# A key-block offset between pairs of heads in a banded-attention tile loop

## The reference

```
q, k, v  = heads of (x @ W.T + b)
zq, zk   = q @ Wproj.T, k @ Wproj.T          # one scalar per row and head
bw       = softplus(log_bandwidth) + 1e-4
ctx[i]   = sum_j max(0, 1 - |zq[i] - zk[j]| / bw) * v[j]     / T
...                                           # expert layer: top 8 of 64 experts,
out      = routed experts + shared expert     # each of capacity 128
```

## Time and profile before

| | |
|---|---|
| median of three runs | 2455.28 us |
| the profiled execution | 2456.26 us |
| its span, first to last instruction | 2455.0 us |
| mean granted clock of TensorE | 0.906 of 2.4 GHz |
| PE busy | 1961.3 us (80%) |
| DVE busy | 2015.5 us (82%) |
| ACT busy | 1923.6 us (78%) |
| POOL busy | 999.9 us (41%) |

### The profile page before, as it was taken

One profiled execution on the slowest core, in us unless ns is written; L12 is line 12 of the kernel. 1 busy time (PEld: TensorE's weight loads), 2 busy tenths in 40 slices (PEclk: granted clock), 3 DMA queues, 4 the chain that ended last, 5 costly groups with the idle time before them and its releaser, 6 DMA issues.

```text
span 2455.0 us, 30185 instructions
## 1 busy us (share of the span) xinstructions
PE 1961.3 (80%) x11666; PEld 779.4 (32%) x11666; DVE 2015.5 (82%) x2895; ACT 1923.6 (78%) x1242; POOL 999.9 (41%) x356
## 2 busy tenths in 40 slices
PE   7788889789669889886788889778898884899920
PEld 4433233233112223221222322112232333677720
DVE  5497888797999998999998989998999986644348
ACT  2398998898999999999999999999999970122223
POOL 1020110100335367364284466342574371276754
PEclk9899999899889999998999999888999995788965
DMA  6315244335120212131202030312111018478779
GB/s 220 131 61 197 84 156 149 122 106 201 57 103 11 88 31 82 41 110 43 95 31 80 20 107 20 123 49 83 50 58 56 20 46 222 108 188 185 179 197 314
DMA packets 182039, 259.26 MB, mean 106 GB/s; under 512 B 22280, under 2 KB 162184, under 8 KB 173704
## 3 DMA queue, kind: packets, MB, share of 16 engines
q1 hardware_dynamic: 167408, 237.83, 29.1%
q0 software_dynamic: 12288, 18.88, 4.5%
q10 hardware_dynamic: 2200, 0.60, 0.1%
HBM read 187.25 MB, written 70.03 MB: 105 GB/s over the span
## 4 chain that ended last, share of the span: by engine, by line
PE 35%; ACT 28%; DVE 24%; POOL 5%; issue 4%; DMA 3%; SPq 1%; DVEq 0%; POOLq 0%; ACTq 0%
ACT TB L1036 28%; PE ps L860 11%; DVE TB L1348 9%; PE ps L766 5%; PE ps L804 4%; DVE TB L1372 4%; PE ps L811 3%; DVE st L1084 2%; PE ps L953 2%; POOL scr L1514 2%; DVE TB L1346 2%; POOL rs L1506 1%; POOL ve L1504 1%; PE ps L914 1%; PE ps L832 1%
## 5 line engine op out<-in xcount | busy, mean ns | idle before, releaser
L1036 ACT ACTIVATE TB<-ZB,nzk 128x2048 f32<-128x2048 f32 x938 | 1794.7, 1994 | 144.4 <-PE ps L860 97.6
L860 PE MATMUL ps<-TB,V 128*32 128x512 f32 x8192 | 1106.0, 641 | 275.6 <-DVE TB L1348 260.0
L1348 DVE TENSOR_SCALAR TB<-TB 128x2048 f32<-128x2048 f32 x938 | 1129.0, 1228 | 101.0 <-ACT TB L1036 98.9
L860 PEld LDWEIGHTS ps<-TB,V 128*32 128x32 f32 x8192 | 208.8, 113 | 1002.8 <-DVE TB L1348 625.0
L1514 POOL TENSOR_TENSOR scr<-ebase,scr 128x256 f32<-128x256 f32 x12 | 509.7, 42471 | 0.0
L1504 POOL TENSOR_SCALAR ve<-mv 128x4 f32<-128x4 f32 x64 | 84.1, 1314 | 837.0 <-DVE mv L1088 837.0
L804 PE MATMUL ps<-XF,wsgu 128*128 128x512 f32 x512 | 259.1, 631 | 1.1 <-DVE TB L1255 0.6
L1372 DVE SCALAR_TENSOR_TENSOR TB<-ZB,kz 128x2048 f32<-128x2048 f32 x86 | 212.2, 2468 | 4.2 <-PE ps L860 4.2
L1512 POOL TENSOR_TENSOR scr<-ebase,scr 128x4 f32<-128x4 f32 x12 | 29.4, 2452 | 388.1 <-DVE scr L1209 388.1
L1063 ACT ACTIVATE ZB<-ps 128x128 f32<-128x128 f32 x64 | 17.7, 277 | 189.7 <-PE ps L953 189.7
L804 PEld LDWEIGHTS ps<-XF,wsgu 128*128 128x128 f32 x512 | 92.2, 197 | 149.3 <-issue 141.9
(11 more groups left out here) (178 smaller groups left out, 1639.2 us busy)
## 6 DMA issues: line engine op xcount, KB each, us to landing
ZB<-zq_rows SPq DMA_DIRECT2D x64, 1024.0 KB, 7.3
scr<-fused_w SPq DMA_DIRECT2D x48, 512.0 KB, 3.5
TB<-in_egu_w SPq DMA_DIRECT2D x44, 256.0 KB, 3.5
y_rows<-zero SPq DMA_DIRECT2D x20, 512.0 KB, 5.1
fused_w<-TB SPq DMA_DIRECT2D x4, 2048.0 KB, 6.7
TB<-y_rows SPq DMA_DIRECT2D x16, 512.0 KB, 8.5
XF<-in_x SPq DMA_DIRECT2D x24, 256.0 KB, 3.2
v_rows<-scr SPq DMA_DIRECT2D x24, 256.0 KB, 2.1
```

The costliest lines, as they stand in the source:

```text
L860: ins = pe.matmul(ps[c][32 * j:32 * j + 32, :], V[:, o:o + 32], tile(t)[:, 512 * c:512 * c + 512], start=(kb == 0), stop=(kb == KB - 1))
L1036: act.activation(tile(e), zrow(head), ACT.Abs, bias=nzk[b][:, kb * H + g:kb * H + g + 1], scale=1.0).then_inc(s_abs, 1)
L1348: dve.tensor_scalar(T, T, 1.0, 1.0, ALU.min, ALU.subtract).then_inc(s_bump, 1)
```

## The change

`ORDER` gives the head and key block of each position: (0,0), (1,0), then for kb = 0 to 14 the four tiles (0,kb+1), (1,kb+1), (2,kb), (3,kb), and last (2,15), (3,15). Every engine reads its tile from it, so heads 0 and 1 of a quad end at positions 58 and 59 rather than 60 and 61, and heads 2 and 3 begin at positions 4 and 5 rather than 2 and 3. The loads of the row buffers are listed at 60, 61, 63 and 64 rather than 61 to 64, the loads of the values of the next batch two positions later, and an own tile may not be the first tile of a head.

```
+def quad_order():
+    o = [(0, 0), (1, 0)]
+    for kb in range(KB - 1):
+        o += [(0, kb + 1), (1, kb + 1), (2, kb), (3, kb)]
+    return o + [(2, KB - 1), (3, KB - 1)]
...
-            if ahead > 15 and 4 <= i < 60:
+            if ahead > 15 and 4 <= i < 60 and ORDER[i][1]:
...
-        sy += [(204 + 4 * kb, "vl", b + 1, kb) for kb in range(KB)]
+        sy += [(206 + 4 * kb, "vl", b + 1, kb) for kb in range(KB)]
...
-            s = 64 * ((n - NZB) % H // 4) + 61 + (n - NZB) % 4
+            s = 64 * ((n - NZB) % H // 4) + (60, 61, 63, 64)[(n - NZB) % 4]
...
-            tiles = [256 * (o // H) + 64 * (o % H // 4) + 4 * kb + o % 4 for kb in range(KB)]
+            tiles = [64 * (o // 4) + i for i in range(64) if ORDER[i][0] == o % 4]
...
-                q, kb, j = t // 64, t // 4 % 16, t % 4
+                q, (j, kb) = t // 64, ORDER[t % 64]
...
-                    if b and n in (0, 32):
-                        pe.wait_ge(q_vl[n // 32], 128 * b)
+                    if b and n in (0, ORDER.index((0, 8))):
+                        pe.wait_ge(q_vl[min(n, 1)], 128 * b)
```

More of the change, by code:

```diff
@@ L26 @@
            "rm": 15, "re": 8, "sc": 14, "sm": 5, "sg": 4, "gu": 7, "dn": 8}
+def quad_order():
[3 more added lines that the diff above has]
+    return o + [(2, KB - 1), (3, KB - 1)]
+ORDER = quad_order()
 def own_tiles():
@@ L590, in sync_stage @@
             elif what == "vl":
-                sp.wait_ge(*tile_used(256 * (b - 1) + 192 + 4 * k + 3))
+                sp.wait_ge(*tile_used(256 * (b - 1) + 192 + ORDER.index((3, k))))
                 for j in range(2):
@@ L1022, in scalar_program @@
                 for n in range(SLOTS):
-                    head = 16 * b + 4 * (n // 64) + n % 4
-                    kb, g = n // 4 % 16, head % H
+                    j, kb = ORDER[n % 64]
+                    head = 16 * b + 4 * (n // 64) + j
+                    g = head % H
                     for e in pace.due(n - 1):
@@ L1343, in vector_program @@
                     if 256 * b + n in own:
-                        o = n // 4 % 16 * H + 4 * (q % 4) + n % 4
+                        o = ORDER[n % 64][1] * H + 4 * (q % 4) + ORDER[n % 64][0]
                         top = kz[:, 1, o:o + 1]
```

## The result

The changed kernel takes 2473.03 us (median of 6 runs, 2466.7 to 2476.84) against 2454.89 us for the kernel before on the same chip: ratio 1.0074, 95% interval 1.0053 to 1.0094. Run again in another set it takes 2475.93 us against 2454.45 us (17 runs): 1.0090, 1.0072 to 1.0109. The order costs 18 to 21 us.

The account below looks back on a forecast made before the run. The loop was taken to run at ACT's pace plus ACT's waits. Costs at quad ends and after the last tile summed to 23.1 us, less 7.7 got back: +15.4 on 2456.26, about 2470 us by the runs, range 2455 to 2490.

Parts of the forecast that it names:

- The price of a doubled step: Steps at quad ends with two matmuls on one strip: 0.86 us more PE time each, 77 us in all.
- The end of quad 1: PE is the bound; steps 62, 63, 0, 3 and 4 add 4.3 us, and earlier query rows give nothing.
- The end of quad 3: Input rows landing earlier give −1.7 us, steps 3 and 4 cost +1.7 us: together 0.
- Quad 4: First batch boundary: steps 62, 63, 0 and 3 cost, the moved own tile gives −1.6 us: together +2.0 us.
- The ends of quads 7, 11 and 15: PE's chain is closed at quad 7, +3.4 us; at 11 and 15 half, 1.7 us each: together 6.9 us.
- The ends of quads 6, 10 and 14: Bank 0 full later, step 3, and half of step 4: 2.1 us each, 6.4 us together.
- The quads forecast at nothing or little: Ends of quads 5, 9, 13 and 12 at 0; ends of quads 2 and 8 at +0.9 us each.
- The third that ACT gets back: ACT's waits for PE, mostly behind DVE's own tiles and stages, shorten when ACT comes later: 7.7 us back.
- That only the quad ends are in PE's chain: Costs were counted end by end, only where they stand in the chain: 23.1 us, including 1.7 after the last tile.
- The rival in which the pauses hide the doubled steps: PE's 275.6 us of waits in L860 absorb the added work: +1.7 to +5 us, 2459 us; chance 0.22.
- The rival in which PE doesn't catch up: The whole 5.2 us at 9 of 15 quad ends, nothing back: +48 us, 2504 us; chance 0.15.
- The rival in which the transfers decide: Same-strip matmuls overlap or their time is waited out; earlier loads give −7.3 us, 2448 us; chance 0.08.

Follow-up runs that it names:

- its own run: Kernel before with only the own tiles 68 and 260 moved to 71 and 263, old tile order and lists: 2453.26 us, 0.9996.
- a kernel that puts them where the pauses are: Kernel before with eight tiles exchanged per quad where PE releases buffers longest before ACT needs them, 96 doubled steps: 2464.10 us, 1.0041.
- least room: Kernel before with eight tiles exchanged per quad where PE releases buffers least ahead of ACT, 96 doubled steps: 2498.38 us, 1.0181.
- both lists of loads: Changed tile order with SP's list of loads as before, against the kernel before: 2474.04 us, 1.0088; with the new list 2475.93 us.
- the four with 288 doubled steps: Executions of the kernel before with eight tiles exchanged at three places of each quad (positions 12, 28 and 44): 2528.63 us, 1.0299.

## Why the prediction was right

The forecast was 2470 us, 15 us more than before; measured are 18 and 21 us more.

*The price of a doubled step*, 0.86 us, taken from a single matmul that took as long as four, is right to 0.06 us wherever a chain at the full clock shows it. The 77 us of the prediction leave out six doubled steps, three at the kernel's start and three after the last tile; with them it is 82. ACT's wait for PE grew by 19.3, 23.7 and 22.0 us in the three traces, where 10 to 25 were forecast.

*The end of quad 1* (4.3 us) measured 4.2 us in the chain and 3.7 us in the quad's length. That the 4.0 us of waiting for query rows bring nothing, because PE is the bound there, is right: the wait went and the quad got longer.

*The end of quad 3* was mis-sized. The input rows did not land sooner, as the row that answers to the earlier trace rows shows:

```profile
473.99 6.15 DMA XF<-in_x
```

6.15 us after 6.10: the −1.7 did not come that way. The quad is 1.1 us shorter on average all the same, by the clock: the piece from the transposes to the step behind them got 2.6 us shorter at the full clock, and doubled steps 3 and 4 took 1.7 us of it.

*Quad 4* got +1.2 instead of +2.0. The steps 62 and 63 are there with 3.56 us for 1.86. The doubled steps 0 and 3, priced at 1.9 us, took no more than the plain ones had taken at the lower clock (1.89 for 2.42 and 1.84 for 1.91). The own tile, priced at −1.6, is worth 0.5 us in the trace of its own run. Two terms were wrong, in opposite directions.

*The ends of quads 7, 11 and 15* were forecast at 3.4, 1.7 and 1.7 us and the last steps at 1.7. Measured are 3.2, 3.8 and 4.5 together with the last steps, 1.7 of which are those steps. Halving 11 and 15 for "some room" was wrong: 3.8 and 2.8 came.

*The ends of quads 6, 10 and 14*, 2.1 each, measured 2.4, 0.2 and 4.8: the sum 6.4 was met with 7.4, the single ones only in one case. That the sum agrees is luck. In quad 10 the full clock gave part of the cost back, and quad 14 cost more than twice its price, by what was not settled.

*The quads forecast at nothing or little* were not all so: quad 2 got +2.3 for 0.9, quad 5 +1.2 for 0, and 8 and 9 together −0.8 for +0.9.

*The third that ACT gets back*, 7.7 us, was the weakest step, and its mechanism did not occur. From position 14 of each quad on, quad 13 left out, ACT waits 51.1 us for PE in the trace before and 53.5, 54.5 and 56.6 us in the three of the changed order: no wait behind own tiles grew shorter in the sum. What came back is the 5.1 us of quad 13 and smaller amounts in quads 3, 4 and 10, by a higher granted clock. Without quad 13 the quads add up to 24.1 us where I had 23.1 before giving back. The size was good and its reason wrong: that the forecast lies as near as it does is in this part luck.

*That only the quad ends are in PE's chain*, on which I built my expectations for the experiments, was wrong as a rule. The terms of the prediction were read from the chains at those ends and hold where those chains were full; the conclusion that elsewhere the work would be hidden was not read anywhere, and cost me four wrong expectations.

The rival in which the pauses hide the doubled steps is real, but only for a kernel that puts them where the pauses are: +9 us. The rival in which PE doesn't catch up is what least room gives, at 2498 us. The rival in which the transfers decide falls: doubled steps cost their 0.8 to 0.9 us, so two matmuls of one strip don't overlap, and both lists of loads give the same time.

## What to carry to other kernels

When small matmuls run side by side on parts of the array, the order of the tiles is also a schedule of those parts. Before reordering, write down which part each matmul of a step takes, and price every collision with the time of one matmul. How much of it shows was told here better by the room at that place, the time between a buffer's release and its next use, than by an engine's busy share: the same number of collisions cost 9 us or 43 us. It is no full rule, since at the end of a quad other waits count as well. And a wait that stands beside the chain, as the one for query rows did, gave nothing when it was removed.

## What the runs showed of the hardware

Four fp32 matmuls of 128 x 32 by 512 columns on four strips take 1.07 us at the full clock, one alone 1.02 us. Where two of the four share a strip, the step takes 0.80 to 0.86 us more, and where both pairs do (steps 63 and 3), no more than that.

The mean granted clock of an execution is 0.902 to 0.915 in the 41 executions of the kernel before that stand beside the experiments, 0.914 to 0.924 in the 18 of the changed order and 0.927 to 0.929 in the four with 288 doubled steps: it was higher where PE had more work. In one quad the stretch at the lower level (0.66 on the mean of 20 us) was gone, which gave 5.1 us back in every trace of the changed order.

PE's busy time in L872 grew by 50.8 us and not by 82 (96 doubled steps of 0.86 us). Most of the difference is the clock: of that busy time 166.4 us fell in stretches at the lower level before and 117.8 us after. With time at the lower level counted half, an estimate, it grew from 1022.8 to 1097.8 us, by 75 us. The rest was not settled.
